# A four-layer recurrent block on one core: late experts' up products moved into the second attention's preparation

## The reference, cut to what matters

```python
xn = layernorm(x);  s = attn_i(xn);  g = silu(ffn_i(xn));  x = x + s * g     # i = 0..3
# 1: attention: causal, 16 heads of 8;   ffn: fp4_linear(silu(gate) * up), values quantised in blocks of 16
# 3: attention: a chunked memory;        ffn: 8 experts, 2 of them weighed by a softmax of the gate's scores
h12 = einsum('btd,ehd->bteh', x, w12)
hidden = silu(h12[..., :H]) * h12[..., H:]
y = sum(total_probs[..., None] * einsum('bteh,edh->bted', hidden, w3), axis=-2)
```

## Time and profile before

| | us |
|---|---|
| median of 3 runs | 3758.95 (3758.35 to 3760.73) |
| the profiled execution | 3768.15 |
| its span | 3766.1 |
| TensorE busy | 3414.2 (91%) |
| VectorE busy | 2487.1 (66%) |
| ScalarE busy | 1798.1 (48%) |
| GpSimd busy | 977.2 (26%) |

### The profile page before, as it was taken

How to read it: one execution, slowest core, us unless ns; L and a number is a source line. 1 busy time by engine, 2 the same in 40 slices (tenths; PEclk the granted TensorE clock), 3 DMA queues, 4 the chain that set the end, 5 groups by cost and what they waited for, 6 DMA issues and landing times. The chain is left out here.

```text
span 3766.1 us, 56142 instructions
## 1 busy us (share of the span) xinstructions
PE 3414.2 (91%) x20181; PEld 1785.1 (47%) x20181; DVE 2487.1 (66%) x5466; ACT 1798.1 (48%) x3832; POOL 977.2 (26%) x845
## 2 busy tenths in 40 slices
PE   7999899989998999988999989989999889999887
PEld 3445534545355544455444553454534554445544
DVE  5576666676566765767656765767656776576676
ACT  3554444544544535545445544445355453554434
POOL 1133311432023410333114330243202341133323
PEclk8999999999999999999999999999999999999998
DMA  5100101102011021000111010110200001100140
GB/s 173 35 18 24 51 23 35 37 4 72 1 35 40 1 72 32 15 29 34 39 35 34 8 66 7 35 40 1 72 19 28 29 28 45 35 16 25 46 111 24
DMA packets 80571, 138.69 MB, mean 37 GB/s; under 512 B 9670, under 2 KB 55910, under 8 KB 77606
## 3 DMA queue, kind: packets, MB, share of 16 engines
q1 hardware_dynamic: 75976, 120.94, 10.1%
q10 hardware_dynamic: 4320, 14.11, 1.2%
HBM read 105.13 MB, written 29.10 MB: 36 GB/s over the span
## 5 line engine op out<-in xcount | busy, mean ns | idle before, releaser
L707 DVE TENSOR_REDUCE nmax<-banks 128x1 f32<-128x512 f32 (+3 forms) x1216 | 760.3, 658 | 337.8 <-PE banks L510 206.7
L627 ACT ACTIVATE probs<-banks 128x512 f32<-128x512 f32 (+3 forms) x1024 | 478.8, 526 | 255.8 <-PE banks L529 148.2
L145 PE MATMUL banks<-filler,identb 128*128 128x512 bf16 x1896 | 495.5, 379 | 9.3 <-PEq L493 9.3
L529 PE MATMUL banks<-qs,ks 74*128 74x512 bf16 (+3 forms) x1536 | 440.7, 328 | 36.2 <-ACT probs L627 13.8
L510 PE MATMUL banks<-ks,qs 72*128 72x512 bf16 (+3 forms) x1536 | 436.9, 329 | 39.0 <-DVE nmax L707 20.2
L510 PEld LDWEIGHTS banks<-ks,qs 72*128 72x128 bf16 x1536 | 140.6, 97 | 312.7 <-DVE nmax L707 162.6
L145 PEld LDWEIGHTS banks<-filler,identb 128*128 128x128 bf16 x1896 | 179.1, 98 | 209.5 <-issue 56.3
L1570 ACT ACTIVATE probs<-banks,nm 128x192 f32<-128x192 f32 x512 | 172.1, 421 | 206.7 <-DVE nm L1522 206.7
L627 ACT ACTIVATE early<-banks 128x256 f32<-128x256 f32 (+3 forms) x512 | 196.5, 438 | 152.4 <-PE banks L529 151.8
L1604 POOL TENSOR_TENSOR probs<-probs,inv 128x768 f32<-128x768 f32 x128 | 187.0, 1466 | 253.6 <-DVE inv L1532 253.6
L529 PEld LDWEIGHTS banks<-qs,ks 74*128 74x128 bf16 x1536 | 141.0, 98 | 222.2 <-ACT probs L627 75.7
(11 more groups left out here) (501 smaller groups left out, 6694.5 us busy)
## 6 DMA issues: line engine op xcount, KB each, us to landing
qs<-parts_scratch SPq DMA_DIRECT2D x300, 96.0 KB
ks<-parts_scratch SPq DMA_DIRECT2D x288, 96.0 KB
parts_scratch<-parts SPq DMA_DIRECT2D x50, 384.0 KB, 2.6
shared<-in_w_h SPq DMA_DIRECT2D x17, 1024.0 KB, 6.8
shared<-in_w SPq DMA_DIRECT2D x26, 256.0 KB, 4.0
layers<-in_layers ACTq DMA_DIRECT2D x1, 3250.0 KB, 24.7
qs<-max_parts SPq DMA_DIRECT2D x192, 4.0 KB
xn<-in_x SPq DMA_DIRECT2D x9, 256.0 KB, 2.8
```

The lines of the kernel that those rows point to most:

```text
L145: nc.tensor.matmul(K.ps[:, bank, :], K.identb[:, :], K.filler[:, :], start=True, stop=True)
L529: mm = nc.tensor.matmul(K.ps[:, b, q0:T], K.ks[0:KR, h, k * P:(k + 1) * P], K.qs[0:KR, h, q0:T], start=True, stop=not on_tensor)
L627: nc.scalar.activation(probs[:, 4 * (q % QUADS) + m % 4, q0:T], K.ps[:, bank("second", m), q0:T], ACT.Exp, scale=scale).then_inc(exped, 1)
L707: nc.vector.tensor_reduce(nmax[:, t, h:h + len(heads)], K.ps[:, n % 2, 0:len(heads) * keys].rearrange("p (j k) -> p j k", k=keys), AX.X, A ...
```

## The change

In the preparation of the second attention the 13 fillers go, and calls of the parts beside stand in new places; the constants of the late experts and the step of the xq transposes are changed; v goes to bank 7 there instead of bank 2.

```diff
 VectorE, prepare
+                if not rms:
+                    beside.run(beside.on_vector, -30)
                 dve.wait_ge(rstd_ready, 1)
...
-                v = K.ps[:, 3 if rms else 2, :].rearrange("p (t h d) -> p t h d", t=NT, d=HD)
+                v = K.ps[:, 3 if rms else 7, :].rearrange("p (t h d) -> p t h d", t=NT, d=HD)
 TensorE, prepare
-                keep_busy(nc, K, 3, 13)
+                if not rms:
+                    beside.run(beside.on_tensor, -29)
                 if rms:
+                    keep_busy(nc, K, 3, 13)
...
                 if not rms:
-                    beside.run(beside.on_tensor, -22)
+                    beside.run(beside.on_tensor, -27)
                     pe.wait_ge(v_used, 1)
-                    beside.run(beside.on_tensor, -21)
+                    beside.run(beside.on_tensor, -26)
                     pe.wait_ge(left, 2)
-                    beside.run(beside.on_tensor, -20)
+                    beside.run(beside.on_tensor, -19)
 ScalarE, prepare
                 else:
+                    beside.run(beside.on_scalar, -29)
                     act.wait_ge(turned, NT)
...
                 if not rms:
-                    beside.run(beside.on_scalar, -22)
+                    beside.run(beside.on_scalar, -28)
 LateExperts
-    UP = -22, -21, -10, -10, -4.5, -2.5
-    DOWN = -9, -2, 1
-    HID = -9.6, -9.6, -7.5, -5.5, -2.5, -1.5
-    ADD = -2.9, -1.2, 1
-    GATE, GATE_READ, SCORES, DONE = -20, -8.5, -1, 8
+    UP = -30, -29, -28, -27, -4.5, -2.5
+    DOWN = -19, -2, 1
+    HID = -30, -29, -9.6, -9.5, -4, -2.4
+    ADD = -7, -1.2, 1
+    GATE, GATE_READ, SCORES, DONE = -20, -9.7, -1, 8
 Fp4ThenExperts
+    XQ_STEP = -26
```

More of the change, by code:

```diff
@@ L337, in _ @@
                 for t in range(NT):
-                    mm = nc.tensor.matmul(K.ps[:, 3 if rms else 2, t * P:(t + 1) * P], srcT[:, t * P:(t + 1) * P],
+                    mm = nc.tensor.matmul(K.ps[:, 3 if rms else 7, t * P:(t + 1) * P], srcT[:, t * P:(t + 1) * P],
                                           wv[:, :], start=True, stop=True)
```

## The result

The change makes the kernel slower: 3778.95 us (median of 5 runs, 3777.43 to 3782.32) against 3760.73 for the kernel before (5 runs, 3758.35 to 3764.64). The ratio is 1.0048, with a 95% interval of [1.0037, 1.006]: +18.2 us, where +14 was forecast. One slow run of experiment 5, 5691 us at a mean granted clock of 0.60, is left out of all that follows.

What follows compares the result with a forecast made beforehand. The prediction took TensorE's own list, not the loads, to set the first scores, with no engine saturated throughout. +4 for the place of the work and +10 for the clock, on the 3759 us median, gave 3773 us, range 3760 to 3784.

Steps and rivals of the forecast that it cites:

- The sum: Whole kernel: +4 for the place of the work and +10 for the clock, +14 us on the median.
- The order on TensorE: Behind v: the call issues nothing; gate, up 2, up 3, down 0 run in one row from 149.75 to 156.4.
- The pause: TensorE between v and the gate: 2.3 us idle, 0.63 busy with transposes, 0.65 idle.
- The +0.9 for the gate: Preparation: the gate's matmuls, which wait for `left`, start at 149.75 instead of 148.86.
- The place of the work: Late experts' work moved ahead of the barrier: first scores at 168.3 against 167.81, +0.5 us per sample, +4 in eight.
- The clock, 6 of 8 samples at 1.7 us: TensorE behind the pause: granted clock falls to 0.50 for 3.4 us in 6 of 8 samples, +10 us, bounds 0 and 27.
- The late store: Factors' store to HBM behind the preparation: 5.2 us later, taken as 0 cost, bound 1 us per sample.
- The margin of 1.8 us for the first loads: First group of loads: in by 166.5, 1.8 us ahead of the first scores.
- The clock did not hold: Rival that the clock holds through TensorE's pause: only +4, 3763 us; chance 0.17.
- The filled gap: Rival: up 2 and up 3 run directly behind v; scores 2.5 us earlier per sample, 3739 us; chance 0.08.
- The binding transfers: Rival: first loads or maxima's rows come late, up to 1 us more per sample, 3781 us; chance 0.05.

Runs made afterwards that it cites:

- experiment 5: Kernel before with only up 0, up 1 and their products moved to the start, fillers out, v in bank 7; 3784.02 us, ratio 1.006.
- experiment 1: Changed kernel with the gate's product behind up 2 and up 3 in the late experts' TensorE generator; 3732.79 us, ratio 0.991 to the kernel before.
- experiment 2: Changed kernel with ten filler matmuls in TensorE's pause behind v, nothing else moved; 3763.99 us, ratio 1.0001 to the kernel before.
- experiment 3: Changed kernel without ScalarE's call at -28, so Silu of up 2 stands behind the second parts; 3777.18 us, ratio 1.0033 to the kernel before.

## Why the prediction was right, and where its terms were off

**The sum.** The order, the pause and the fall of the clock were foreseen, and experiments 1 and 2 show that they make the loss. That the sum came near is in part luck. At the first scores of all eight samples the place of the work, put at +4, gave -0.8; the clock, put at +10, gave +13.2; and waits for the first loads, put at 0, gave +0.85. The errors cancel: 13.3 against a forecast of 14.

**The order on TensorE** was read rightly: gate, up 2, up 3, down 0 in a row behind `left`, and nothing at the call behind v. Experiment 1 is the same kernel without that order, at a ratio of 0.991 instead of 1.0048.

**The pause** was forecast as 2.3 idle, 0.63 busy, 0.65 idle; the trace has 2.50, 0.63, 0.55. The +0.9 for the gate that leads to it came out as +0.8 (11.96 us behind the block's start against 11.18).

**The place of the work, +0.5 per sample:** this term failed. Experiment 2 and the first sample of experiment 3 give -0.1. Half of the error of 0.6 is a sum of modelled lengths: the gate, up 2 and up 3 together, and down 0 count 1.16 + 3.6 + 1.95 = 6.7 us, but from the gate's start to down 0's end they took 6.4 in experiment 2, since each starts 0.15 to 0.2 us before the modelled end of the one before. The rest is in small pieces of 0.1 us, at the gate and behind the barrier. The barrier in experiment 3 opened 18.67 us behind the block's start, I had 19.0; the second fp4 product came 2.53 us behind it, I had 2.65.

**The clock, 6 of 8 samples at 1.7 us:** the mechanism was right, the price holds in the mean and the count was low. There were eight falls. Against 30.08, the scores with the clock held, and without the waits for loads, they cost 13.2 us, 1.65 each in the mean, but they are not alike: the seven of 3.4 us cost 1.25 to 1.67, and the one of 6.8 us cost 2.7. The scores of all samples together come 13.3 us later than before (mean 31.8 against 30.2). In experiment 3, with the same pause, there were six falls, 1.64 us each in the mean. So six and eight were seen, and the count differs between executions.

The Trainium skill, page "TensorE: Matmul & The Clock Gate", section "HAM oscillation — how this bites in real kernels", has the same mechanism: groups with waits between them start cold. These traces agree for most samples: in the changed kernel the low clock had begun before the gate in six of the eight, and in the other two it began 0.4 us into it (the gate took 1.74 us there, not 2.08). Part 4, "PE-mode transpose", of the same page of the Trainium skill says that transposes do not count as busy in the way that other matmuls do. With four transposes in the pause the clock fell in eight of eight samples, as the prediction drew from that, but in experiment 3 in only six of eight. No run here has the pause with and without transposes, so whether they matter stays open.

**The late store, 0 with a bound of 1 us per sample:** this term was too low. The shift was forecast as +5.2 without a fall; it was +4.8 in experiment 2 (third parts at 16.04 us behind the block's start against 11.25) and +6.3 with a fall (155.35 in the timeline above). The margin of 1.8 us for the first loads was not there in every sample. In the sixth and the seventh of the changed kernel the first scores waited for them:

```profile
2404.68 0.38 PE L515 MATMUL banks<-ks,qs 72*128 72x128 bf16 x4 [0.40 <-DMA ks<-parts_scratch]
2849.84 0.38 PE L515 MATMUL banks<-ks,qs 72*128 72x128 bf16 x4 [0.45 <-DMA ks<-parts_scratch]
```

The second scores came 3.1 us later behind the first, over the eight samples, than in the kernel before. Half of that is the first sample, 1.6 us and so above the bound. There the clock fell behind this wait as well, for longer than in any preparation:

```profile
186.91 0.94 PE L534 MATMUL banks<-qs,ks 74*128 74x512 bf16 x2 [2.13 <-DMA qs<-max_parts]
```

```profile
183.50:187.00 3.50, 1.37 (x10) 0.67 (x9) 1.58 (x3) 2.86 (x4) 1.71 (x2) 1.00 0.11 40
187.00:197.00 10.00, 10.00 (x34) 3.96 (x35) 4.54 (x8) 4.13 (x8) 3.36 (x4) 0.50 0.00 0
```

The wait had been 0.49. That sample is the longest, 450.5 us against 443.3 before. Of its 7.2 us, 1.4 are at the first scores and 1.6 in this wait; the remaining 4.1 are about what the long fall would cost (half of 10 us is 5). But the wait does not always bring it. In the seventh sample of experiment 2 the same wait was as long, and the clock stayed at 1.00:

```profile
2850.86 0.61 PE L535 MATMUL banks<-qs,ks 74*128 74x512 bf16 x2 [2.10 <-DMA qs<-max_parts]
...
2850.80:2860.80 10.00, 9.55 (x70) 5.03 (x70) 7.61 (x14) 5.65 (x14) 4.18 (x5) 1.00 0.00 0
```

So 13.3 of the 18.2 us are accounted for at the first scores. In the one profiled execution the second scores add 3.1 and the long fall 4.1, and falls at other places differ in both directions. How the 4.9 us that are left of the medians divide among these is not shown.

**The rivals.** The clock did not hold. The filled gap was the right picture of the other order, and undersized: 20 us less than the kernel before were forecast, experiment 1 measured 31.6 less (3732.79 against 3764.35). The binding transfers are a small part of the loss at the first scores and a larger one behind them, and the coming bound of the faster kernels.

## What to carry to other kernels

Count an engine's idle time at the place where work is taken away, not only where it is put: the up products cost TensorE nothing at the block's start, but they had been the only thing between v and the gate. Where order is set by due steps, follow what each part's own sequence lets out first; a smaller number does not overtake the piece ahead of it. To tell clock from place, fill the pause with matmuls that nobody reads and change nothing else.

## What the runs showed of the hardware

The same pause of 2.50 and 0.55 us, at the same place of the same program, was followed by the granted clock at 0.50 in some samples and at 1.00 in others, so its price has to be counted over samples and not read from one. TensorE groups in a row overlap by 0.15 to 0.2 us of their modelled lengths at each seam, which was half of the error of one term. And a wait of 2.13 us for a transfer was followed by 10 us at the lower clock, with TensorE busy throughout, where the pauses of 3 us in the preparation were mostly followed by 3.4 us; a wait of 2.10 us at the same place, in experiment 2, was followed by no fall.
